# Values, projection and resampling of a second attention in halves, and the next batch's keys through another PSUM bank

## The chip, the cores and the metric

One core of a Trainium2 chip runs the whole program in one launch. The metric is device time in microseconds (us), lower is better. The engines are TensorE (PE in the profile; PEld its weight loads), VectorE (DVE), ScalarE (ACT), GpSimd (POOL) and SyncE (SP, which issues DMAs). Each engine runs its own stream of instructions in order, and the streams are tied together by semaphores.

## What is computed

The reference is a chain of layers over x of shape (4, 256, 256): a conditioned attention, a second attention, a resampling along the channels, a sparsified feed-forward, a GRU over time, a third attention and a routed feed-forward. The change touches the second attention and the resampling behind it:

```python
def _L0_attn_ref(x, W_qkv, W_out, b_out):
    B, S, H = x.shape
    ...
    q8, q_scale = act_quant(q)
    k8, k_scale = act_quant(k)
    scores = jnp.einsum('bhqd,bhkd->bhqk', q8.astype(jnp.float32), k8.astype(jnp.float32))
    scores = scores * (q_scale * k_scale) / jnp.sqrt(jnp.float32(hd))
    attn = jax.nn.softmax(scores, axis=-1)
    v8, v_scale = act_quant(v)
    out = jnp.einsum('bhqk,bhkd->bhqd', attn, v8.astype(jnp.float32))
    out = out * v_scale
    out = out.transpose(0, 2, 1, 3).reshape(B, S, H)
    return jnp.einsum('bsh,ho->bso', out, W_out) + b_out
...
x = x + _L0_attn_ref(_L0_cond_ref(...), L0_attn_W_qkv, L0_attn_W_out, L0_attn_b_out)
x = x + _L0_ffn_ref(_L0_cond2_ref(x, cond_2048, 1, 1), ...)
```

act_quant rounds to an 8-bit float with one scale for the whole tensor. There are 4 batches of 256 tokens and 16 heads of size 16. `_L0_cond2_ref` interpolates linearly between two channels, at places that the condition gives; the kernel does it as a product with a 256x256 matrix for each batch.

## The kernel before

Every engine has one function for the second attention (`phase2_pe`, `phase2_act`, `phase2_pool`, `phase2_dve`), and the order of each stream is written out by hand: a loop over H, the head counted over all batches (0 to 63), with conditions on h = H % 16, the head in its batch b. Some lines ahead of H run 8 heads early (LEAD = 8).

On TensorE, one step H issues, in this order:

- `scores(H + 8)`: two 16-bit products (L938, 32 rows of the array) into one of three banks. VectorE's `top` takes their maxima (L1204, into nraw).
- `by_key(H)`: the same scores with the keys on the partitions (L962), into one of two banks. ScalarE takes the exponential (L1098) into one of eight buffers, work or probs_b. A bank is free again when its exponential is done, so `by_key(H)` waits for the exponential of H-2.
- `rows_again` at H % 4 = 2: two transposes (L948) into bank pY, which bring the queries of the next four heads (a group) back with their maxima beside them. It waits for GpSimd's `split` of that group's maxima (L1156 to L1159). VectorE copies the result out (`rows_out`, L1210), and the group's `by_key` waits for that.
- `values` at H % 4 = 1: probabilities times values of the group before, 8 products of 32-bit numbers (L975) into pR.
- `heads_in(b + 1, side)` at h = 0 (queries) and 2 (keys): 8 transposes each (L924) into pX, copied out by ScalarE's `heads_out` (L1062).
- the chain of the batch before: `out_rows` at h = 3 and 5 (transposes, L990), `out_cols` at h = 7 (L997), `projected` at h = 9 (8 passes of 32-bit product, L1013) and `resample` at h = 12 (L1005). All go through pX. Between them VectorE normalises (L1215, L1218), ScalarE copies (L1077) and VectorE adds the projection to xT (L1224); ScalarE's `regather` copies the resampling out (L1072).

After the loop the last batch's values, output chain and resampling follow, and then the next stage (L1325), which needs all four batches. `keep_warm(n, bank)` issues n products of zeros (L307).

GpSimd's stream in a batch is `split` of the four groups, with the rounding of the next batch's queries, keys and values between them (`pushed`, `rounded_v`, `rounded_qk`); VectorE makes the bit masks for it (`exponents`, L1196 and L1197).

## Time and profile before

| | us |
|---|---|
| median of 3 timed runs | 1082.24 (1080.93 to 1088.04) |
| profiled execution, its own time | 1084.97 |
| its span | 1083.2 |
| TensorE busy in the span | 855.8 (79%) |
| VectorE, ScalarE, GpSimd busy | 674.9, 494.8, 391.7 |
| second attention, from the first by-key product to the next stage | 213.18 to 314.96 |

The times are of whole executions; the span is the part that the profile covers. The second attention is about a tenth of it. The other stages are the same in both kernels.

### The profile page before, as it was taken

Reading aid. Unit: us, or ns where it says so; the run is one execution under the profiler, and the core shown is the slowest. Engines: PE = TensorE matmul, PEld = TensorE weight load, DVE = VectorE, ACT = ScalarE, POOL = GpSimd, SP = SyncE. Lnnn points to the kernel's source line nnn. Section 1 sums busy time; section 2 is a strip of 40 time slices with the busy share of each in tenths; the row PEclk is TensorE's granted clock in tenths of the full one; section 3 lists DMA queues with packets and bytes.
Section 4 is the critical chain, followed back from the end, with each engine's and each line's share of the span. In section 5 each row is a group of like instructions: output and inputs, shape, how many; then the busy total and the mean of one; then the engine's idle time right before and its main releaser. Section 6 shows DMA issues by size and latency. Waiting matters only on the chain.

```text
span 1083.2 us, 39645 instructions
## 1 busy us (share of the span) xinstructions
PE 855.8 (79%) x16359; PEld 544.3 (50%) x16359; DVE 674.9 (62%) x2314; ACT 494.8 (46%) x1987; POOL 391.7 (36%) x473
## 2 busy tenths in 40 slices
PE   3778777788989786969688796967766899999717
PEld 3444443344545464546455464645444567667506
DVE  5644544756434576676667676666766567667573
ACT  2423333456531465656565465655555435435201
POOL 0476550454316294674829285670020000000000
PEclk9999999959899898999999899999999899999768
DMA  8000000400000000000000000000200000000101
GB/s 258 6 1 1 2 1 1 145 2 2 1 20 8 6 6 11 4 14 4 14 4 13 4 4 13 5 14 4 51 34 4 2 1 0 0 0 0 40 0 39
DMA packets 32519, 20.00 MB, mean 18 GB/s; under 512 B 23136, under 2 KB 29280, under 8 KB 32352
## 3 DMA queue, kind: packets, MB, share of 16 engines
q1 hardware_dynamic: 27168, 17.04, 5.6%
q8 instruction: 123, 2.02, 0.8%
q10 hardware_dynamic: 5184, 0.59, 0.4%
q14 instruction: 44, 0.36, 0.1%
HBM read 14.47 MB, written 1.05 MB: 14 GB/s over the span
## 4 chain that ended last, share of the span: by engine, by line
PE 59%; DVE 23%; ACT 7%; issue 6%; POOL 0%; DMA 0%; ACTq 0%; DVEq 0%; POOLq 0%
PE banks L1378 15%; PE banks L1325 5%; PE banks L322 4%; DVE work L1661 4%; DVE gate_r L1657 4%; DVE h_ring L1675 3%; PE banks L1348 3%; ACT nzh L1507 3%; DVE pre_n L1666 3%; PE banks L1690 3%; PE banks L307 3%; PE banks L336 2%; PE banks L551 2%; PE banks L523 2%; PE banks L975 2%
## 5 line engine op out<-in xcount | busy, mean ns | idle before, releaser
L1378 PE MATMUL banks<-w_qkv,h_ring 128*4 128x64 f32 x12288 | 228.1, 223 | 111.0 <-DVE h_ring L1675 98.2
L1378 PEld LDWEIGHTS banks<-w_qkv,h_ring 128*4 128x4 f32 x12288 | 178.5, 89 | 214.4 <-DVE h_ring L1675 197.2
L1498 ACT ACTIVATE banks<-gate_r 128x8 f32<-128x8 f32 x256 | 46.2, 180 | 182.0 <-DVE gate_r L1657 182.0
L307 PE MATMUL banks<-zero 128*128 128x512 bf16 x360 | 113.0, 395 | 2.0 <-PE banks L461 2.0
L1657 DVE STREAM_TRANSPOSE gate_r<-banks 128x64 f32<-128x64 f32 x256 | 64.0, 250 | 79.3 <-PE banks L1378 75.5
L1661 DVE STREAM_TRANSPOSE work<-banks 128x64 f32<-128x64 f32 x256 | 76.6, 299 | 2.9 <-PE banks L1378 2.6
L1675 DVE TENSOR_TENSOR_SCAN h_ring<-banks,nzh 128x24 f32<-128x24 f32 x256 | 52.9, 207 | 32.4 <-ACT nzh L1507 0.8
L1666 DVE TENSOR_TENSOR_SCAN pre_n<-banks,work 128x16 f32<-128x16 f32 x256 | 48.7, 190 | 26.9 <-DVE work L1661 0.9
L1668 DVE STREAM_TRANSPOSE banks<-gate_z 128x64 f32<-128x64 f32 x256 | 60.4, 236 | 6.0 <-ACT gate_z L1503 4.8
L1532 POOL TENSOR_TENSOR work<-work 128x512 f32<-128x512 f32 x14 | 17.8, 1271 | 125.1 <-ACT work L1435 125.1
L1503 ACT ACTIVATE gate_z<-banks 128x64 f32<-128x64 f32 x256 | 57.1, 223 | 11.0 <-PE banks L1378 10.6
L1507 ACT ACTIVATE nzh<-pre_n 128x8 f32<-128x8 f32 x256 | 54.5, 213 | 15.7 <-DVE pre_n L1666 1.0
L375 ACT ACTIVATE probs_b<-banks,nraw 128x128 f32<-128x128 f32 (+1 forms) x128 | 46.8, 417 | 32.5 <-DVE nraw L386 31.5
L1204 DVE TENSOR_REDUCE nraw<-banks 128x2 f32<-128x512 f32 x64 | 42.6, 687 | 29.1 <-PE banks L938 29.1
L322 PE MATMUL banks<-shared,qT 128*128 128x128 f32 (+1 forms) x256 | 59.1, 343 | 0.0
L1458 ACT COPY banks<-big 128x64 f32<-128x64 f32 x256 | 54.1, 211 | 9.3 <-DMA big<-big 9.3
L307 PEld LDWEIGHTS banks<-zero 128*128 128x128 bf16 x360 | 34.1, 98 | 42.4 <-issue 10.5
L1458 ACT COPY banks<-grids 128x64 f32<-128x64 f32 x256 | 54.0, 211 | 0.0
L1458 ACT COPY banks<-bhn 128x64 f32<-128x64 f32 x256 | 54.0, 211 | 0.0
L1625 DVE TENSOR_TENSOR nzh<-h_ring,banks 128x16 f32<-128x16 f32 x256 | 43.9, 171 | 12.2 <-ACTq L1494 3.0
L1603 POOL COPY xnT<-h_ring 128x128 f32<-128x128 f32 x16 | 7.2, 482 | 122.0 <-DVE h_ring L1675 122.0
L1726 POOL COPY aT<-xnT 128x256 f32 (+1 forms) x10 | 3.7, 400 | 117.7 <-PE banks L1690 117.4
(394 smaller groups left out, 1820.2 us busy)
## 6 DMA issues: line engine op xcount, KB each, us to landing
big<-in_x SPq DMA_DIRECT2D x1, 1024.0 KB, 5.8
w_gate<-in_L_ffn_w_gate SPq DMA_DIRECT2D x1, 1024.0 KB, 5.0
shared<-in_L_ffn_w_down SPq DMA_DIRECT2D x1, 1024.0 KB, 7.6
w_gate<-in_L_ffn_W SPq DMA_DIRECT2D x1, 1024.0 KB, 7.0
shared<-in_L_ffn_W SPq DMA_DIRECT2D x1, 1024.0 KB, 6.6
out_x<-big SPq DMA_DIRECT2D x4, 256.0 KB, 2.2
w_qkv<-in_L_cond_W_qkv SPq DMA_DIRECT2D x1, 768.0 KB, 7.0
w_qkv<-in_L_attn_W_qkv SPq DMA_DIRECT2D x1, 768.0 KB, 8.7
```

Of the source, the lines that this page charges most:

```text
L307: nc.tensor.matmul(bank[:, :], zero16[:, 0:P], zero16[:, :], start=True, stop=True, skip_group_check=True)
L322: nc.tensor.matmul(pSQ[h % 3][:, o:o + n], qT[:, c, tile], k[:, c, 0:n], start=True, stop=False, skip_group_check=True)
L1325: mm = nc.tensor.matmul(bank[:, :], xg[:, tile, k, :], w_gate[:, k, n * 512:(n + 1) * 512] if not up else w_up[2 * k + n], start=(k == 0), ...
L1378: mm = nc.tensor.matmul(bank[32 * j:32 * j + B, 0:64], h_col(t, c), w_hh[:, c, g, :].rearrange("p (m n) -> p m n", m=KC)[:, :, 32 * j:32 * ...
L1458: return nc.scalar.copy(bank[:, 0:64], rows).then_inc(done, 1)
L1503: nc.scalar.activation(gate_z[:, :], bank_z[:, 0:64], ACT.Sigmoid, scale=-1.0).then_inc(g_sz, 1)
L1507: nc.scalar.activation(every(nzh[:, :], 0, 3), every(pre_n[:, :], 1), ACT.Tanh, scale=-1.0).then_inc(g_th, 1)
L1657: nc.vector.transpose(gate_r[:, :], bank_r[:, 0:64]).then_inc(g_tr, 1)
L1661: nc.vector.transpose(blocks(npair[:, 16 * (t % RING):16 * (t % RING) + 128], 0), bank_n[:, 0:64].rearrange("p (m n) -> p m n", m=KC)).the ...
L1666: nc.vector.tensor_tensor_scan(pre_n[:, :], zr[:, :], npair[:, 16 * (t % RING):16 * (t % RING) + 16], 0.0, ALU.mult, ALU.add).then_inc(g_p ...
L1668: nc.vector.transpose(blocks(zz[:, :], 2, 3), gate_z[:, :].rearrange("p (m n) -> p m n", m=KC)).then_inc(g_tz, 1)
L1675: nc.vector.tensor_tensor_scan(h_ring[:, h_at(t + 1):h_at(t + 1) + 24], zz[:, 0:24], nzh[:, :], 0.0, ALU.mult, ALU.subtract).then_inc(g_h, 1)
```

## The change

In the second attention:

- `values`, `projected` and `resample` are issued in two halves, under two neighbouring heads: values at H % 4 = 1 and 2, projection at h = 11 and 12, resampling at h = 7 and 8.
- The keys of the next batch come in at h = 3 in place of 2, and through pY (the bank of the rows), after VectorE's copy of the group's rows. `rows_again` of the third group waits for ScalarE's copy of the keys.
- The output chain of the batch before begins two heads later: out_rows at h = 5 and 7, out_cols at h = 9.
- Resampling is done for the batch two before, from batch 2 on, into pY. So the resamplings of batches 2 and 3 both stand after the loop, the first of them in place of three warm-up products. `rows_again` of the fourth group waits for its copy.
- The lead-in has one warm-up product in place of two under heads 4 to 7.
- In batch 0 GpSimd takes `split` of the second group ahead of the rounding of values; VectorE's masks move from h = 2 to 1 and from 8 to 11.

The diff, without most of its unchanged lines:

```diff
@@ -912,12 +912,13 @@
 
...
             def heads_in(b, side):
-                pe.wait_ge(p_qk, b + 1)
-                if side and b:
-                    pe.wait_ge(p_tc, 2 * b + 1)
-                elif b >= 3:
-                    pe.wait_ge(e_xgc, b - 2)
-                out = pR if side and b == 0 else pX
+                out = (pR if b == 0 else pY) if side else pX
+                if side == 0:
+                    pe.wait_ge(p_qk, b + 1)
+                    if b >= 3:
+                        pe.wait_ge(p_x, b - 2)
+                elif b:
+                    pe.wait_ge(a_re, Q + 4 * b - 2)
                 for g in range(4):
...
                         h0 = side * NH + 4 * g
@@ -933,7 +934,8 @@
                     pe.wait_ge(a_max, Q + H - 2)
...
                     pe.wait_ge(p_tc, 2 * b + 2)
-                keep_warm(2 if H < LEAD else 0, bank[H % 3])
+                if H < LEAD:
+                    keep_warm(2 if H < 4 else 1, bank[H % 3])
                 for t in range(ST):
...
                                           start=True, stop=True, skip_group_check=True)
@@ -944,6 +946,10 @@
                 pe.wait_ge(p_split, G + 1)
...
                     pe.wait_ge(a_re, Q + G)
+                if g == 2 and b + 1 < B:
+                    pe.wait_ge(p_tc, 2 * b + 4)
+                if g == 3 and b >= 2:
+                    pe.wait_ge(e_xgc, b - 1)
                 for t in range(ST):
...
                                              ident16[:, :])
@@ -963,26 +969,27 @@
                                           start=True, stop=True, skip_group_check=True)
...
 
-            def values(G):
+            def values(G, t):
                 b, g = divmod(G, 4)
-                pe.wait_ge(a_exp, Q + 4 * G + 4)
-                if g == 0:
-                    pe.wait_ge(p_v8, b + 1)
-                if g % 2 == 0 and G:
-                    pe.wait_ge(a_oqc, 2 * B + G // 2)
-                for t in range(ST):
-                    for j in range(4):
-                        mm = nc.tensor.matmul(pR[32 * j:32 * j + 32, (g % 2) * S:(g % 2 + 1) * S], vs[b % 2][:, t, 4 * g + j, :],
-                                              prob[(4 * G + j) % 8][:, t * S:(t + 1) * S], start=(t == 0), stop=(t == ST - 1), skip_group_check=True)
-                mm.then_inc(a_v, 1)
+                if t == 0:
+                    pe.wait_ge(a_exp, Q + 4 * G + 4)
+                    if g == 0:
+                        pe.wait_ge(p_v8, b + 1)
+                    if g % 2 == 0 and G:
+                        pe.wait_ge(a_oqc, 2 * B + G // 2)
+                for j in range(4):
+                    mm = nc.tensor.matmul(pR[32 * j:32 * j + 32, (g % 2) * S:(g % 2 + 1) * S], vs[b % 2][:, t, 4 * g + j, :],
+                                          prob[(4 * G + j) % 8][:, t * S:(t + 1) * S], start=(t == 0), stop=(t == ST - 1), skip_group_check=True)
+                if t == ST - 1:
+                    mm.then_inc(a_v, 1)
 
...
                     if b + 2 < B:
-                        pe.wait_ge(p_tc, 2 * b + 6)
+                        pe.wait_ge(p_tc, 2 * b + 5)
                     else:
-                        pe.wait_ge(e_xgc, b)
+                        pe.wait_ge(p_x, b)
                 elif b + 1 < B:
...
                 out = bank[0] if t and b == B - 1 else pX
@@ -997,22 +1004,26 @@
                         mm = nc.tensor.transpose(pX[:, c * S + t * P:c * S + (t + 1) * P], o_sb[:, t, c * P:(c + 1) * P], ident)
...
 
-            def resample(b, out):
-                pe.wait_ge(e_gm, b + 1)
-                pe.wait_ge(p_x, b + 1)
-                for m in range(KC):
-                    for k in range(KC):
-                        mm = nc.tensor.matmul(out[:, m * S:(m + 1) * S], gmats[b][:, k, m * P:(m + 1) * P], xT[:, k, b * S:(b + 1) * S],
-                                              start=(k == 0), stop=(k == KC - 1), skip_group_check=True)
-                mm.then_inc(e_xg, 1)
-
-            def projected(b):
-                pe.wait_ge(a_otc, B + b + 1)
-                for m in range(KC):
-                    for k in range(KC):
-                        mm = nc.tensor.matmul(pX[:, m * S:(m + 1) * S], w_out2[:, k, m * P:(m + 1) * P], oT[:, k, :],
-                                              start=(k == 0), stop=(k == KC - 1), skip_group_check=True)
-                mm.then_inc(p_proj, 1)
+            def resample(b, out, m):
+                if m == 0:
+                    pe.wait_ge(e_gm, b + 1)
+                    pe.wait_ge(p_x, b + 1)
+                    if b + 2 < B:
+                        pe.wait_ge(a_re, Q + 4 * b + 11)
+                for k in range(KC):
+                    mm = nc.tensor.matmul(out[:, m * S:(m + 1) * S], gmats[b][:, k, m * P:(m + 1) * P], xT[:, k, b * S:(b + 1) * S],
+                                          start=(k == 0), stop=(k == KC - 1), skip_group_check=True)
+                if m == KC - 1:
+                    mm.then_inc(e_xg, 1)
+
+            def projected(b, m):
+                if m == 0:
+                    pe.wait_ge(a_otc, B + b + 1)
+                for k in range(KC):
+                    mm = nc.tensor.matmul(pX[:, m * S:(m + 1) * S], w_out2[:, k, m * P:(m + 1) * P], oT[:, k, :],
+                                          start=(k == 0), stop=(k == KC - 1), skip_group_check=True)
+                if m == KC - 1:
+                    mm.then_inc(p_proj, 1)
 
...
             nc.tensor.transpose(pX[0:3, 0:P], amax3[:, :], ident).then_inc(s_gmax, 1)
@@ -1031,27 +1042,32 @@
                     by_key(H)
...
                     rows_again((H + 2) // 4)
-                if H % 4 == 1 and H > 4:
-                    values(H // 4 - 1)
-                if b >= 0 and b + 1 < B and h in (0, 2):
-                    heads_in(b + 1, h // 2)
-                if b >= 1 and h in (3, 5):
-                    out_rows(b - 1, (h - 3) // 2)
-                if b >= 1 and h == 7:
+                if H % 4 in (1, 2) and H > 4:
+                    values(H // 4 - 1, H % 4 - 1)
+                if b >= 0 and b + 1 < B and h in (0, 3):
+                    heads_in(b + 1, h // 3)
+                if b >= 1 and h in (5, 7):
+                    out_rows(b - 1, (h - 5) // 2)
+                if b >= 2 and h in (7, 8):
+                    resample(b - 2, pY, h - 7)
+                if b >= 1 and h == 9:
                     out_cols(b - 1)
-                if b >= 1 and h == 9:
-                    projected(b - 1)
-                if b >= 1 and h == 12:
-                    resample(b - 1, pX)
-            values(4 * B - 1)
-            keep_warm(3, bank[1])
+                if b >= 1 and h in (11, 12):
+                    projected(b - 1, h - 11)
+            for t in range(ST):
+                values(4 * B - 1, t)
+            for m in range(KC):
+                resample(B - 2, bank[3], m)
             for t in range(ST):
...
             out_cols(B - 1)
-            projected(B - 1)
+            keep_warm(3, bank[1])
+            for m in range(KC):
+                projected(B - 1, m)
             keep_warm(6, bank[1])
-            resample(B - 1, pY)
+            for m in range(KC):
+                resample(B - 1, pY, m)
             pe.wait_ge(e_xg, B)
...
             phase3_pe(pe)
@@ -1059,7 +1075,7 @@
         def phase2_act(act):
...
                 act.wait_ge(p_t, 2 * b + side + 1)
-                nc.scalar.copy((qT16s, kT16s)[side][b % 2].rearrange("p g s -> p (g s)"), pX.bitcast(BF16)).then_inc(p_tc, 1)
+                nc.scalar.copy((qT16s, kT16s)[side][b % 2].rearrange("p g s -> p (g s)"), (pX, pY)[side].bitcast(BF16)).then_inc(p_tc, 1)
 
...
                 act.wait_ge(a_v, Q + 4 * b + 2 * n + 2)
@@ -1096,17 +1112,18 @@
                 if H >= 8:
...
                 nc.scalar.activation(prob[H % 8], bank[3 + H % 2], ACT.Exp, scale=sscale[:, 0:1]).then_inc(a_exp, 1)
-                if b + 1 < B and h in (0, 2):
-                    heads_out(b + 1, h // 2)
-                if b >= 1 and h == 1:
+                if b + 1 < B and h in (0, 3):
+                    heads_out(b + 1, h // 3)
+                if b >= 1 and h == 2:
                     out_of_groups(b - 1, 1)
-                if h == 9:
+                if b >= 2 and h == 8:
+                    regather(b - 2, pY)
+                if b >= 1 and h == 9:
+                    out_cols_out(b - 1)
+                if h == 10:
                     out_of_groups(b, 0)
-                if b >= 1 and h == 7:
-                    out_cols_out(b - 1)
-                if b >= 1 and h == 12:
-                    regather(b - 1, pX)
             out_of_groups(B - 1, 1)
+            regather(B - 2, bank[3])
             out_cols_out(B - 1)
...
             regather(B - 1, pY)
@@ -1164,16 +1181,20 @@
                 split(4 * b)
...
                     pushed(0, 2, 3)
-                    rounded_v(0)
-                if b + 1 < B:
+                elif b + 1 < B:
                     pushed(b + 1, 2, 3)
                 split(4 * b + 1)
-                if b + 1 < B:
+                if b == 0:
+                    rounded_v(0)
+                    pushed(1, 2, 3)
+                elif b + 1 < B:
                     rounded_v(b + 1)
...
                 split(4 * b + 3)
+                if b == 0:
+                    rounded_v(1)
                 if b + 2 < B:
...
             pool.wait_ge(p_v8, B)
@@ -1258,15 +1279,15 @@
                 if H in (-6, -3):
...
                     exponents((H + 6) // 3, 2, 3, p_ev)
-                if b >= 0 and b + 2 < B and h == 2:
+                if b >= 0 and b + 2 < B and h == 1:
                     v.wait_ge(p_y, b + 2)
                     exponents(b + 2, 0, 2, p_e)
-                if b >= 0 and b + 2 < B and h == 8:
+                if b >= 0 and b + 2 < B and h == 11:
                     v.wait_ge(p_yv, b + 3)
                     exponents(b + 2, 2, 3, p_ev)
-                if b >= 1 and h in (4, 6):
-                    out_normalised(b - 1, (h - 4) // 2)
-                if b >= 1 and h == 10:
+                if b >= 1 and h in (6, 8):
+                    out_normalised(b - 1, (h - 6) // 2)
+                if b >= 1 and h == 13:
                     projected_out(b - 1)
...
```

TensorE's stream in batch 1, before, from the second `out_rows` to the values under head 9 (L938 scores, L962 by key, L948 rows, L990 and L997 transposes of the output, L975 values):

```order
199 L990 MATMUL banks<-cst,work 128x128 x4
200 L938 MATMUL banks<-shared,qT 128x256 x2
201 L962 MATMUL banks<-shared 128x256 x2
202 L948 MATMUL banks<-ident,qkp 128x128 x2
203 L938 MATMUL banks<-shared,qT 128x256 x2
204 L962 MATMUL banks<-shared 128x256 x2
205 L997 MATMUL banks<-cst,o_sb 128x128 x4
206 L938 MATMUL banks<-shared,qT 128x256 x2
207 L962 MATMUL banks<-shared 128x256 x2
208 L938 MATMUL banks<-shared,qT 128x256 x2
209 L962 MATMUL banks<-shared 128x256 x2
210 L975 MATMUL banks<-probs_b,work 32x256 x8
```

The changed kernel, same batch, from the rows under head 6 to out_cols (L940 scores, L968 by key, L954 rows, L997 and L1004 transposes, L981 values):

```order
205 L954 MATMUL banks<-ident,qkp 128x128 x2
206 L981 MATMUL banks<-work 32x256 x4
207 L940 MATMUL banks<-shared,qT 128x256 x2
208 L968 MATMUL banks<-shared 128x256 x2
209 L997 MATMUL banks<-cst,work 128x128 x4
210 L940 MATMUL banks<-shared,qT 128x256 x2
211 L968 MATMUL banks<-shared 128x256 x2
212 L940 MATMUL banks<-shared,qT 128x256 x2
213 L968 MATMUL banks<-shared 128x256 x2
214 L981 MATMUL banks<-probs_b,work 32x256 x4
215 L1004 MATMUL banks<-cst,o_sb 128x128 x4
```

The values stood whole under heads 5 and 9, with both transposes between; now a half stands under head 6 too, and out_cols follows the half under head 9.

TensorE's stream after the last head, before (L1325 is the next stage):

```order
308 L975 MATMUL banks<-probs_b,work 32x256 x8
309 L307 MATMUL banks<-zero 128x512 x3
310 L990 MATMUL banks<-cst,work 128x128 x8
311 L307 MATMUL banks<-zero 128x512 x3
312 L997 MATMUL banks<-cst,o_sb 128x128 x4
313 L1013 MATMUL banks<-oT,w_out 128x256 x4
314 L307 MATMUL banks<-zero 128x512 x6
315 L1005 MATMUL banks<-xT,h_ring 128x256 x4
316 L1325 MATMUL banks<-w_gate,xnT 128x512 x2
```

The changed kernel there (L1014 resampling, L1023 projection, L1346 the next stage):

```order
330 L981 MATMUL banks<-probs_b,work 32x256 x8
331 L1014 MATMUL banks<-xT,h_ring 128x256 x4
332 L997 MATMUL banks<-cst,work 128x128 x8
333 L307 MATMUL banks<-zero 128x512 x3
334 L1004 MATMUL banks<-cst,o_sb 128x128 x4
335 L307 MATMUL banks<-zero 128x512 x3
336 L1023 MATMUL banks<-oT,w_out 128x256 x4
337 L307 MATMUL banks<-zero 128x512 x6
338 L1014 MATMUL banks<-xT,h_ring 128x256 x4
339 L1346 MATMUL banks<-w_gate,xnT 128x512 x2
```

The resampling of batch 2 took the place of the first three warm-up products, and three more stand ahead of the projection.

GpSimd's stream in batch 0, before, from the first group's split on (L1156 to L1159 split, L1131 and L1147 values):

```order
53 L1159 TENSOR_TENSOR qkp<-nraw,qkp 128x2x4
54 L1131 TENSOR_TENSOR big<-big,grids 128x256 x2
55 L1147 TENSOR_TENSOR v_sb<-big,grids 128x16x16 x2
56 L1131 TENSOR_TENSOR big<-big,grids 128x256 x2
57 L1156 TENSOR_TENSOR qkp<-nraw,zero 128x2x4
```

The changed kernel there (L1173 to L1176 split, L1148 and L1164 values):

```order
53 L1176 TENSOR_TENSOR qkp<-nraw,qkp 128x2x4
54 L1148 TENSOR_TENSOR big<-big,grids 128x256 x2
55 L1173 TENSOR_TENSOR qkp<-nraw,zero 128x2x4
56 L1174 TENSOR_TENSOR nraw<-nraw,qkp 128x2x4
57 L1175 TENSOR_TENSOR qkp<-nraw,zero 128x2x4
58 L1176 TENSOR_TENSOR qkp<-nraw,qkp 128x2x4
59 L1164 TENSOR_TENSOR v_sb<-big,grids 128x16x16 x2
```

The second split moved ahead of two of the three pieces of work on the values.

## Rows read from the trace of the kernel before

**Rows 1.** Stretches: batches 0 to 3 and tail; us, busy (instructions), PEclk

```profile
213.18:235.64 22.46, 18.24 (x139) 7.77 (x139) 14.20 (x25) 12.27 (x19) 14.65 (x29) 0.59 0.01 1
235.64:260.78 25.14, 22.93 (x181) 12.50 (x180) 15.42 (x31) 14.91 (x23) 11.45 (x25) 0.82 0.01 1
260.78:283.40 22.62, 20.41 (x183) 11.91 (x182) 13.14 (x27) 14.12 (x23) 4.99 (x18) 0.92 0.00 1
283.40:303.86 20.46, 17.39 (x145) 9.10 (x141) 8.12 (x18) 12.85 (x21) 9.56 (x14) 0.92 0.01 2
303.86:314.96 11.10, 9.19 (x57) 5.66 (x57) 2.27 (x6) 3.24 (x5) 0.71 (x1) 1.00 0.00 1
```

**Rows 2.** Waits of TensorE in batch 2: total us, times, longest

```profile
PE banks L997 <- DVE o_sb L1218: 0.7, 1, 0.7
PE banks L990 <- ACT shared L1062: 0.7, 1, 0.7
PE banks L1005 <- DVE xT L1224: 0.4, 1, 0.4
PE banks L990 <- DVE o_sb L1218: 0.2, 1, 0.2
```

**Rows 3.** Timeline of TensorE in batch 0: start, us, what, idle before

```profile
217.01 0.28 PE L948 MATMUL banks<-ident,qkp 128*128 128x128 bf16 x2 [2.28 <-POOL qkp L1159]
...
225.34 0.60 PE L962 MATMUL banks<-shared 32*128 32x256 bf16 x2 [0.59 <-ACT probs_b L1098]
```

**Rows 4.** Timeline of TensorE in batches 1 and 2

```profile
243.20 0.40 PE L938 MATMUL banks<-shared,qT 32*128 32x256 bf16 x4
...
243.75 1.07 PE L975 MATMUL banks<-work 128*32 128x256 f32 x16
...
249.53 1.94 PE L975 MATMUL banks<-probs_b,work 128*32 128x256 f32 x16
...
261.87 1.07 PE L975 MATMUL banks<-probs_b,work 128*32 128x256 f32 x16
...
263.53 0.61 PE L924 MATMUL banks<-ident,qkp 128*128 128x128 bf16 x8
...
266.44 1.07 PE L975 MATMUL banks<-work,v_sb 128*32 128x256 f32 x16
...
271.53 1.70 PE L975 MATMUL banks<-probs_b,v_sb 128*32 128x256 f32 x16
273.16 3.00 PE L1013 MATMUL banks<-oT,w_out 128*128 128x256 f32 x8
...
278.34 1.96 PE L1005 MATMUL banks<-xT,w_emb 128*128 128x256 f32 x8 [0.40 <-DVE xT L1224]
```

**Rows 5.** Stretches of half a microsecond in which the clock changes

```profile
217.00:217.50 0.50, 0.49 (x7) 0.49 (x8) 0.17 (x1) 0.00 (x0) 0.50 (x1) 0.72 0.00 0
...
241.00:241.50 0.50, 0.50 (x8) 0.38 (x7) 0.50 (x2) 0.20 (x2) 0.02 (x1) 0.89 0.00 0
...
247.50:248.00 0.50, 0.31 (x3) 0.31 (x4) 0.50 (x2) 0.23 (x1) 0.00 (x0) 0.94 0.00 0
...
271.50:272.00 0.50, 0.50 (x10) 0.31 (x12) 0.50 (x1) 0.50 (x2) 0.34 (x3) 0.83 0.00 0
...
292.00:292.50 0.50, 0.50 (x7) 0.14 (x5) 0.15 (x1) 0.20 (x1) 0.23 (x1) 0.81 0.00 0
```

**Rows 6.** Timeline of TensorE behind the last values

```profile
304.86 0.82 PE L307 MATMUL banks<-zero 128*128 128x512 bf16 x3
```

**Rows 7.** Timeline of GpSimd in batch 0: split of the second group

```profile
215.82 0.23 POOL L1156 TENSOR_TENSOR qkp<-nraw,zero 128x8 bf16<-128x8 f32 x1
```

**Rows 8.** Groups of VectorE, 205 to 315: busy us, mean ns, idle before

```profile
L1204 DVE TENSOR_REDUCE nraw<-banks 128x2 f32<-128x512 f32 x64 | 42.6, 687 | 29.1 <-PE banks L938 29.1
...
L1218 DVE SCALAR_TENSOR_TENSOR o_sb<-banks,scl,rinv 128x256 f32<-128x256 f32 x8 | 3.9, 484 | 0.3
...
L1196 DVE TENSOR_SCALAR grids<-big 128x1024 int32<-128x1024 int32 x2 | 1.4, 682 | 0.0
```

## The prediction

> **What bounds the kernel now.** The change touches only the second attention, so I first cut its stretch of the span into its four batches with the table of stretches [rows 1]. Its columns give each engine's busy time and, as PEclk, the mean share of full clock that TensorE was granted: 1.00 is 2.4 GHz, 0.50 is 1.2 GHz. In every batch TensorE is the busiest engine by far: 22.93 of 25.14 us in batch 1, against 15.42 on VectorE and 14.91 on ScalarE. What isn't busy on TensorE is 4.2, 2.2, 2.2 and 3.1 us in batches 0 to 3. The list of waits splits batch 2's: 0.7 + 0.7 + 0.4 + 0.2 = 2.0 us, all of them on the side chain (rows of the output, columns, projection, resampling), none on the exponentials [rows 2]. So the bound inside the batches is TensorE's own work, plus these waits.
>
> The second thing that the table shows is the clock. It averages 0.59, 0.82, 0.92 and 0.92. A stretch of length T at mean clock c holds T(1-c) of lost time if TensorE is busy throughout: 22.46 x 0.41 = 9.2 us in batch 0, 25.14 x 0.18 = 4.5 in batch 1, 22.62 x 0.08 = 1.8 in batch 2, 20.46 x 0.08 = 1.6 in batch 3. Together 17.1 us, more than all waits. Fine stretches place it [rows 5]: the clock falls near 217, is back near 241, and falls again near 248, 272 and 292.
>
> What did TensorE do before a fall? The timeline says [rows 4]: values (L975, 32-bit, 1.07 us at full clock) start at 243.75 and next at 249.53; between their end and the next start lie 4.7 us of 16-bit products and transposes, and the clock fell in them. Between 267.5 and 271.53 it is 4.0 us: it fell. Between 262.9 and 266.44 it is 3.5 us: it didn't. The fall at 292 lies in the same part of batch 3: between the values of heads 5 and 9, where a batch has its transposes of the output and one of its two longest waits. The fall at 217 follows 2.28 us without any work, in which TensorE waited for GpSimd's split of the second group's maxima [rows 3].
>
> **The change part by part.**
>
> *Values in halves.* The work is the same, in two pieces under neighbouring heads. At full clock two heads' scores and products by key take 0.55 us (243.20 to 243.75, [rows 4]) and one whole values block 1.07. The products by key run at most two heads ahead of the exponentials, so a whole block leaves ScalarE without input, and TensorE then waits for ScalarE: 0.59 us at 225.34 [rows 3], about once in each group of batch 0. The list of waits of batch 2 has no exponential in it, so the halves save no wait there. The cost of a split is the start of one more block: a block lasts 1.07 us where its steady part is 1.00, so 0.07 for each of some seven splits in a batch: +0.5 us. Below zero is excluded there, since no wait is named that it could remove; above, a split also parts two heads that now overlap (two heads 0.55 us, a head alone about 0.54 to 0.55 with its fill), at most 7 x 0.25 = 1.8 us more. I take 0.5, as most heads of a batch already have a block between them.
>
> *Keys through pY, later output chain.* The keys' transposes no longer go through pX, so the first out_rows needn't wait for ScalarE's copy of the keys: -0.7 us in batches 1 and 2 [rows 2]. out_cols now stands behind half a values block (0.53 us) and, in batches 2 and 3, behind half a resampling: its 0.7 us wait goes in those and falls to about 0.2 in batch 1. Resampling no longer follows the projection that it had to see through VectorE: -0.4. out_rows of the second tile keeps its wait; VectorE's chain from the scores of head 14 (maximum 0.69, product 0.48 [rows 8], and two short operations between them, some 1.8 us in all) against TensorE's 1.45 in between (0.55 for head 15, 0.55 for what is left of head 14, 0.3 of rows and 0.5 of values, less the overlap) gives about 0.35 in place of 0.2. New waits: the keys' transposes at head 3 wait for VectorE's copy of the group's rows, and the bit masks of batches 2 and 3 (two passes of 0.68 us [rows 8]) now stand ahead of that copy in batches 0 and 1: some 0.5 us in batch 1 at full clock. ScalarE waits for the second half of resampling before it goes on to the exponential of head 9; ScalarE has 8 us of slack in a batch (14.1 of 22.6 busy [rows 1]), so I cost that at nothing; without that cover it is 0.35 us in each of two batches. Sum of waits: batch 1 -1.0, batch 2 -1.6, batch 3 -1.2 (it has no heads to bring in; 0.7 of out_cols and 0.2 of the resampling go, and part of the 1.3 us for the last exponentials).
>
> *Resampling two batches late.* One block of 1.96 us [rows 4] leaves batch 1 and lands in the tail: batches 2 and 3 still carry one each. Batch 1: -2.0. In the tail it takes the place of three warm-up products (0.82 us, [rows 6]) between the last values and out_rows, which could start no earlier since they waited for ScalarE's copy of the last groups: 1.96 - 0.82 = +1.15, and +0.1 for the warm-up products now ahead of the projection: +1.25. The end of this stage, 314.96 [rows 1], is what the next stage waits for, so all of it counts.
>
> *Clock in the batches.* In batch 1 the changed stream has between the second values half (head 6) and the next half (head 9): three heads at 0.55, one block of transposes (0.6, as the keys' at 263.53) and its wait of 0.35, that is 2.6 us. Between heads 2 and 5 it is three heads and the keys' transposes (0.6), 2.3 us. In batches 2 and 3 two halves of resampling fill heads 7 and 8. No stretch without 32-bit products is as long as any after which the clock fell, or as the 3.5 us after which it didn't, so I expect the falls of batches 1 to 3 to go: -1.7, -1.7 and -1.6. The long one of batch 0 follows the 2.28 us without work. GpSimd now does split(1) ahead of the values' rounding; it started at 215.82 [rows 7] and could start at about 213.8, when VectorE has its maximum. But VectorE's masks, moved up to head 1, take 1.4 us [rows 8] before the copy of the rows, so the keys' transposes and by-key products of the second group come at about 217.4 as before, and TensorE is idle for some 2 us there all the same; and four heads of the lead-in lose half of their warm-up products. So that fall stays. In half-clock stretches TensorE gained only where full-array 32-bit work and transposes stood close, as at 241; with two heads_in blocks and two halves within heads 0 to 3 of batch 1, this can come earlier. Batch 1 now has 5.4 us at half clock at its start (235.64 to 241), 2.7 us of them lost: the term lies between 0 and -2.7, I take -0.9, nearer to no change, as batch 0's values alone never brought it back.
>
> *Batch 0.* The 0.59 us waits for the exponentials go in part, and the 2.28 us wait is partly replaced: between 0 and -2.5, I take -0.6, the size of one such wait.
>
> **The sum.** Batch 0 -0.6. Batch 1: -1.0 -2.0 -1.7 -0.9 +0.5 = -5.1. Batch 2: -1.6 -1.7 +0.5 = -2.8. Batch 3: -1.2 -1.6 +0.5 = -2.3. Tail +1.25. Total -9.5 us. On the profiled execution's own 1084.97 us that is 1075.5. This execution lies 2.7 above the median of the three timed ones, 1082.24; from the median it is 1072.7. I predict 1073.
>
> **The rivals.**
>
> *The falls stay* (chance 0.22). The stretch before a fall may be counted otherwise than by its 32-bit products: the values at 261.87 and 266.44 lay in a stretch as thin as the one that fell. Then the terms -1.7, -1.7, -1.6 and -0.9 go, and 3.6 us are left: 1078.6. For it: ahead of the falls at 248 and 272 TensorE did stand still for 0.7 us [rows 2]. Against it: the spacing of the three falls. The Trainium skill ("TensorE: Matmul & The Clock Gate", section on why this matters for your kernels) ties a lower clock to long idle gaps between bursts of products; by that rule no fall here is explained, since the clock falls after idle of 0.7 us at most in batches 1 and 2, and rearranging busy work would give this rival's 1078.6.
>
> *The clock does better* (0.18). If TensorE, getting its rows for the second group some 2 us earlier, doesn't fall at 217, or is back in the middle of batch 0, half of that batch's 9.2 us is saved: 1073 - 4.6 = 1068. Against: the idle time ahead of 217.4 as worked out.
>
> *New waits eat the old* (0.12). pY now serves rows, keys and resampling; each change of hands crosses VectorE or ScalarE. With the 1.8 us of parted heads in place of 0.5 in one or two batches and 0.35 to 0.5 us per hand-over, 4 us are lost: 1077.
>
> *Slower* (0.08). The halves thin out TensorE's stream, so the clock, once down in batch 0, isn't granted again at 241. Batch 1's work is 25.14 - 2.2 (waits) - 4.5 (clock) - 2.0 (resampling) = 16.4 us at full clock; done at half clock it costs 16.4 more, where the forecast has 1.8 and the waits of 1.2 vanish: +13.4, 1086. It decides against the change from about 11 us of work at half clock, which is about head 10 of batch 1. If batch 2's 18.6 us run so too, it is 1103. Against: the projection, now in halves at heads 11 and 12, is as dense as at 273, where the clock came back.
>
> **How the numbers follow.** The forecast has 0.40. Its own spread, from the bounds above, is about 1068 to 1079. A measurement of this kernel can't tell changes of less than about 1%, 10.8 us: below 1071.4 is faster, above 1093 slower. Faster: all but a little of the better clock (0.16) and 0.18 of the forecast's 0.40, 0.34. Slower: 0.05, the part of the slower case that runs on into batch 2, and a little of the new waits. The rest, 0.61, is within 1%. For 8 in 10 the range runs from the better clock with a margin, 1064, to short of the slower case, 1083.
>
> **What the changed profile would show.** Mean clock of batches 1 to 3 above 0.95 and no fall between heads 5 and 9 (clock term right); idle time of TensorE near 1.2, 0.4 and 1.9 us (waits right); the stage's last resampling some 12.4 us behind the last exponential's end in place of 11.2 (tail right). A clock still at half at head 8 of batch 1, or idle time ahead of the keys' transposes, would make the prediction wrong.

## The result, and the profile after

The changed kernel took 1112.94 us (median of 4, 1111.88 to 1116.07), the kernel before beside it 1085.14. The ratio is 1.0257, 95% interval [1.0197, 1.0316]: 28 us slower, where 9 us less were forecast. Ratios here and below leave out executions more than 1.5% above the fastest of the same kernel; medians and ranges keep them. The profiled execution took 1111.88, its span is 1110.1.

The same table of stretches as [rows 1], cut at the same places of the program (batches 0 to 3, then past the stage's end at 340.09):

```profile
213.00:235.62 22.62, 19.58 (x138) 7.34 (x138) 14.58 (x25) 12.38 (x18) 15.38 (x29) 0.51 0.01 2
235.62:266.73 31.11, 31.09 (x174) 13.73 (x173) 16.60 (x31) 14.19 (x21) 11.72 (x25) 0.50 0.00 1
266.73:298.12 31.39, 31.39 (x152) 15.06 (x150) 11.66 (x22) 13.51 (x20) 4.93 (x18) 0.50 0.00 1
298.12:327.99 29.87, 27.56 (x174) 11.66 (x173) 11.14 (x23) 14.85 (x23) 9.55 (x14) 0.65 0.00 1
327.99:340.00 12.01, 10.79 (x63) 7.19 (x64) 2.27 (x6) 3.83 (x6) 0.61 (x1) 1.00 0.00 1
```

The clock is 0.50 in batches 1 and 2 and 0.65 in batch 3, where it was 0.82, 0.92 and 0.92. Batch 0 is as long as before. TensorE is busy for all of the 31.39 us of batch 2: no wait is left in the list, only slow work (the ends of products are modelled in the profile, so busy doesn't mean at its peak). The list of waits of TensorE for 213 to 328:

```profile
PE banks L968 <- ACT work L1114: 1.5, 2, 0.8
PE banks L968 <- ACT probs_b L1114: 1.5, 2, 0.8
PE banks L925 <- DVE shared L1231: 1.5, 1, 1.5
PE banks L968 <- DVE shared L1231: 1.1, 1, 1.1
PE banks L981 <- ACT probs_b L1114: 0.8, 1, 0.8
```

None of the waits of [rows 2] is there; the 1.5 us wait for VectorE ahead of the keys' transposes in batch 0 is the one that the prediction feared. Half-microsecond stretches give the fall and the return, as in [rows 5]:

```profile
213.00:213.50 0.50, 0.50 (x6) 0.29 (x7) 0.50 (x2) 0.07 (x1) 0.00 (x0) 0.99 0.00 0
213.50:214.00 0.50, 0.50 (x8) 0.47 (x5) 0.50 (x2) 0.50 (x1) 0.23 (x2) 0.50 0.00 0
...
319.00:319.50 0.50, 0.50 (x3) 0.32 (x1) 0.00 (x0) 0.00 (x0) 0.50 (x1) 0.70 0.00 0
319.50:320.00 0.50, 0.50 (x4) 0.11 (x2) 0.00 (x0) 0.19 (x1) 0.50 (x2) 1.00 0.00 0
```

So the clock was at 1.2 GHz from 213.5 to 319, 106 us, against some 34 before (217 to 241, and three falls). The timeline of TensorE in batch 2 shows the densest work that didn't bring it back (L1014 resampling behind transposes, L1023 projection), and in batch 3 what it had just done when it came back (L1014 again):

```profile
280.19 1.11 PE L997 MATMUL banks<-cst,work 128*128 128x128 f32 x4
281.10 1.91 PE L1014 MATMUL banks<-xT,w_emb 128*128 128x256 f32 x4
...
283.90 2.08 PE L1014 MATMUL banks<-xT,w_emb 128*128 128x256 f32 x4
...
292.19 2.08 PE L1023 MATMUL banks<-oT,w_out 128*128 128x256 f32 x4
294.20 0.60 PE L940 MATMUL banks<-shared,qT 32*128 32x256 bf16 x2
294.60 0.63 PE L968 MATMUL banks<-shared 32*128 32x256 bf16 x2
295.15 2.08 PE L1023 MATMUL banks<-oT,w_out 128*128 128x256 f32 x4
...
314.75 1.11 PE L997 MATMUL banks<-cst,work 128*128 128x128 f32 x4
315.66 1.91 PE L1014 MATMUL banks<-xT,w_emb 128*128 128x256 f32 x4
317.50 0.60 PE L968 MATMUL banks<-shared 32*128 32x256 bf16 x2
318.04 1.74 PE L1014 MATMUL banks<-xT,w_emb 128*128 128x256 f32 x4
```

The same transposes and halves of the resampling stood in batch 2 without a return and in batch 3 ahead of one. So what TensorE had just done doesn't settle by itself when the clock comes back.

The stage ends at 340.09 in place of 314.96, 25.1 us later. The rest of the program is 770.0 us long, 768.2 before.

### The profile page after: what moved, and what is told of

Its sections match the earlier page's. It is cut to its first block, busy times and chain, and to the rows that moved or that the text cites. A ratio compares the mean times of both kernels' runs of the same rounds, so it can differ in the third digit from the quotient of the medians.

```text
span 1110.1 us, 39535 instructions
## 1 busy us (share of the span) xinstructions
PE 855.6 (77%) x16255; PEld 550.9 (50%) x16355; DVE 678.0 (61%) x2314; ACT 496.3 (45%) x1987; POOL 392.3 (35%) x473
## 4 chain that ended last, share of the span: by engine, by line
PE 60%; DVE 20%; ACT 6%; issue 5%; SPq 2%; DMA 2%; ACTq 0%; DVEq 0%; POOL 0%; POOLq 0%
PE banks L1399 13%; PE banks L1346 5%; PE banks L322 4%; DVE work L1682 3%; PE banks L1369 3%; DVE h_ring L1696 3%; DVE gate_r L1678 3%; PE banks L981 3%; ACT nzh L1528 3%; PE banks L1711 3%; PE banks L307 3%; DVE pre_n L1687 2%; SPq L1326 2%; PE banks L336 2%; PE banks L940 2%
## 5 line engine op out<-in xcount | busy, mean ns | idle before, releaser
L307 PE MATMUL banks<-zero 128*128 128x512 bf16 x256 | 74.8, 392 | 3.9 <-PE banks L461 2.6
```

The costliest lines, as they stand in the source:

```text
L307: nc.tensor.matmul(bank[:, :], zero16[:, 0:P], zero16[:, :], start=True, stop=True, skip_group_check=True)
```

## The experiments

Each line of measurement gives the median, the ratio to the kernel before on the same chip with its interval, and from the profiled execution where the clock changed and where the stage ended (first product of the next stage). The profile shows one execution only; for the others there is the mean clock of the whole program.

### Which half does it

The changed kernel with whole values:

```diff
-                if H % 4 in (1, 2) and H > 4:
-                    values(H // 4 - 1, H % 4 - 1)
+                if H % 4 == 1 and H > 4:
+                    for t in range(ST):
+                        values(H // 4 - 1, t)
```

> The changed kernel, but the values of a group are issued whole again under H % 4 = 1 (projection and resampling stay in halves). Theory A: it is the values' halves that keep the clock down, since 1.87 us of 32-bit products in a row at half clock, next to the transposes of the keys or queries, were what stood ahead of the clock's return at 241 in the kernel before. Then the clock is back in batch 1, near 241, the mean clock of batch 1 is 0.75 or more, and the time is 1075 to 1090. Theory B: it is the projection and the resampling, taken apart or taken out of batch 1; then this kernel stays at half clock to batch 3, 1108 to 1118. Theory C: the clock stays down because the lead-in has fewer warm-up products and the fall comes earlier; then this one too stays near 1112.

Measured 1083.72 us, 0.9983 [0.9926, 1.0040]; fall at 213, return at 247, a second fall from 284.5 to 288, stage end 312.99. Theory A's return came; theory C fell, since the first fall was as early and the lead-in the same.

The changed kernel with whole projection and resampling:

```diff
-                if b >= 2 and h in (7, 8):
-                    resample(b - 2, pY, h - 7)
+                if b >= 2 and h == 7:
+                    for m in range(KC):
+                        resample(b - 2, pY, m)
...
-                if b >= 1 and h in (11, 12):
-                    projected(b - 1, h - 11)
+                if b >= 1 and h == 11:
+                    for m in range(KC):
+                        projected(b - 1, m)
```

> The changed kernel, but the projection is issued whole under head 11 and the resampling whole under head 7 (values stay in halves). Theory A (values' halves alone): no return before the projection of batch 1; if the whole projection (4 us at half clock) brings it back, near 262, the time is 1090 to 1100, and if not 1112. Theory B (projection and resampling in halves): the clock is back at the projection of batch 1, 1085 to 1098. Theory C (lead-in): 1112.

Measured 1086.31 us, 0.9974 [0.9934, 1.0014]; return at 261.5, a second fall at 288.5 with the clock back only at 298.5, stage end 318.51 (this profiled execution was the longest of the eight, 1094.84). So neither kind of halves keeps the clock down by itself: with blocks of either kind whole it came back. The mean clocks of all executions say the same: 0.934 to 0.948 with whole values, 0.927 to 0.945 with whole projection and resampling, against 0.904 to 0.915 in the changed kernel.

The kernel before with halved values (ScalarE's copies of them come one head later, which isn't shown here):

```diff
-                if H % 4 == 1 and H > 4:
-                    values(H // 4 - 1)
+                if H % 4 in (1, 2) and H > 4:
+                    values(H // 4 - 1, H % 4 - 1)
```

> The kernel before, with the values alone in halves under H % 4 = 1 and 2 (and ScalarE's copies of them one head later). Theory A: the clock doesn't return at 241; the whole projection of batch 1 may bring it back some 15 us later. Half clock for 15 us more costs about 7 us: 1088 to 1097, or 1110 if it stays down. Theory B and theory C: as before, the clock returns at 241 and the time is 1080 to 1088.

Measured 1098.69 us (2 runs), 1.0128 [0.9893, 1.0362], which settles no difference in time; in the profile the return moved from 241 to 262.5, just behind the whole projection of batch 1 (3.78 us from 257.94), the clock fell twice more (276 to 286.5 and 296.5 to 310), and the stage ended at 329.20. The late return alone proves little: further down, a kernel with whole values has its first return at 260. What the three returns had behind them, in the timelines of whole values (first), whole projection (second) and the kernel before with halved values (third):

```profile
243.71 1.93 PE L981 MATMUL banks<-work 128*32 128x256 f32 x16
245.57 1.12 PE L997 MATMUL banks<-cst,work 128*128 128x128 f32 x4
```

```profile
256.55 3.78 PE L1023 MATMUL banks<-oT,w_out 128*128 128x256 f32 x8
```

```profile
257.94 3.78 PE L1014 MATMUL banks<-oT,w_out 128*128 128x256 f32 x8
```

The reader is to compare them with the projection above: the same products, 2.08 us twice with 1.0 us of 16-bit products on 32 rows between, gave no return.

### Is the clock the whole loss

12 more warm-up products in the changed kernel, in batch 0:

```diff
+                if H == 12:
+                    keep_warm(12, bank[H % 3])
```

> The changed kernel with 12 more warm-up products in a row ahead of the scores of head 12, some 5 us at half clock in batch 0. If the clock is the whole loss: it comes back near 223, the schedule of the change then runs at full clock, and the time is 1065 to 1078, under the kernel before. If thin work also makes it fall again (the halves are too thin to hold it), the mean clock of batches 1 to 3 stays under 0.8 and the time is 1090 or more.

Measured 1115.15 us (2 runs), 1.0280 [1.0108, 1.0451]. The clock did come back, at 224, and held with halves for 10 us; then TensorE waited 1.51 us for GpSimd's split of batch 1's first group, the clock fell at 234 and came back at 319.5; the stage ended at 341.06:

```profile
224.50:234.00 9.50, 7.26 (x88) 2.88 (x84) 7.98 (x13) 7.42 (x12) 5.52 (x11) 1.00 0.01 2
234.00:234.50 0.50, 0.00 (x0) 0.00 (x0) 0.50 (x2) 0.03 (x1) 0.36 (x2) 0.87 0.00 0
234.50:319.50 85.00, 83.14 (x448) 36.80 (x448) 39.83 (x74) 35.62 (x53) 22.58 (x59) 0.50 0.00 1
```

The same burst at the start of batch 1:

```diff
+                if H == 24:
+                    keep_warm(12, bank[H % 3])
```

> The changed kernel, all halves kept, with 12 more warm-up products in a row at the start of batch 1 (ahead of the scores of head 24), some 5 us at half clock. The burst in batch 0 brought the clock back at 224, but it fell again at 234, where TensorE waited 1.5 us for GpSimd, and the halves then didn't bring it back. Theory (halves can't win the clock back, but can hold it): here it is back near 241 and stays to the end of the stage, mean clock of batches 2 and 3 over 0.95; the time is 1076 to 1086. Rival (halves can't hold it either): another fall in batch 1 or 2 without a wait of 1 us ahead of it, and 1100 or more.

Measured 1085.73 us, 0.9953 [0.9912, 0.9994]; return at 240.5, no fall for the rest of the stage, end 311.79, though the burst itself took 5.0 us:

```profile
240.50:241.00 0.50, 0.50 (x3) 0.00 (x0) 0.00 (x0) 0.00 (x0) 0.00 (x0) 0.83 0.00 0
241.00:311.79 70.79, 66.02 (x563) 35.46 (x563) 40.05 (x79) 44.66 (x69) 26.10 (x54) 1.00 0.00 1
```

One burst of zeros takes back all 28 us. With the clock up, the same halves kept it for 70 us; with the clock down, they went 85 us (burst in batch 0) and 106 us (no burst) without it. That they can never win it back isn't shown: both returns near 319 came in halves.

The same with 8 products in place of 12 (`keep_warm(8, bank[H % 3])`):

> The changed kernel with a burst of 8 warm-up products at the start of batch 1 in place of 12. If the return needs only some 3 us of full-array products together with the transposes behind them: as with 12, 1.5 us less, 1078 to 1086. If 8 are too few: no return before batch 3, 1110 to 1116.

Measured 1085.58 us, 0.9948 [0.9909, 0.9987]; return at 239, end 310.17. Three of its ten executions were more than 1.5% above the fastest: 1099.76 and 1101.33 us at mean clocks of 0.933 and 0.922, and 1119.43 us at 0.905, like the changed kernel. In that one 8 products seem not to have been enough; it has no profile.

### What the order is worth without the halves

The changed kernel with values, projection and resampling all whole (both diffs above):

> The changed kernel's order and banks, but values, projection and resampling all whole (heads H % 4 = 1, 11 and 7). Theory (the halves are the whole loss, the rest of the change is worth a little): 1078 to 1088, the clock back at 241 to 247, the stage's end within 3 us of the run with the values whole alone. Rival (the new order itself costs): 1092 or more with the same clock as the kernel before.

Measured 1084.39 us (3 runs), 0.9938 [0.9863, 1.0014]; return at 247, one fall from 261 to 267.5, end 312.11. The new order without the halves shows no cost.

Whole up to head 31, halves behind it:

```diff
+                if H < 2 * NH:
+                    for t in range(ST):
+                        if H % 4 == 1 and H > 4:
+                            values(H // 4 - 1, t)
+                elif H % 4 in (1, 2):
+                    values(H // 4 - 1, H % 4 - 1)
...
-                if b >= 1 and h in (11, 12):
+                if b == 1 and h == 11:
+                    for m in range(KC):
+                        projected(b - 1, m)
+                elif b >= 2 and h in (11, 12):
```

> The changed kernel with the values whole up to head 31 and the projection whole in batch 1, in halves afterwards. Theory (halves are harmful only while the clock is down): the clock is back at 241 to 247 as with whole values, holds, and the time is 1076 to 1084. Rival (halves make the clock fall again and then keep it down): mean clock of batch 2 or 3 under 0.8, 1090 or more.

Measured 1087.07 us, 0.9959 [0.9913, 1.0005]; return at 248, a fall at 261, a return at 275, then no fall, end 316.45. The fall came less than 1 us behind the start of the first half (260.43), at the place where the kernel with everything whole fell too. Neither branch came out as put. Ahead of the return at 275 stood only halves and transposes (at half clock 1.11 us of transposes from 271.40 and 1.91 us of resampling from 272.30), so in this profile work in halves did win the clock back, 14 us after the fall.

### Waits and thin work

The kernel before with four warm-up products under head 7 of batches 1 to 3:

```diff
-                keep_warm(2 if H < LEAD else 0, bank[H % 3])
+                keep_warm(2 if H < LEAD else 4 if H >= NH and h == 15 else 0, bank[H % 3])
```

> The kernel before with four more warm-up products under head 7 of batches 1 to 3, ahead of the transposes that wait 0.7 us for VectorE. Theory (each fall near 248, 272 and 292 follows thin work between heads 5 and 9, and costs some 1.6 us): the falls go, each burst costs 0.2 to 0.9 us, so 1080 to 1084 and mean clock of batches 2 and 3 over 0.97. Rival (the falls follow the place of the batch in time, not the work): they stay, and the time is 1086 to 1090.

Measured 1090.12 us, 0.9972 [0.9925, 1.0019]: no difference. In the profile the first return came late, at 260, but behind it no fall followed to the stage's end at 318.82. Up to 249.5 this kernel issues the same work as the kernel before, with all its whole values blocks, yet its clock did not come back at 241. Lines of its timeline:

```profile
245.44 1.94 PE L975 MATMUL banks<-work 128*32 128x256 f32 x16
247.31 1.12 PE L990 MATMUL banks<-cst,work 128*128 128x128 f32 x4
...
249.50 1.91 PE L307 MATMUL banks<-zero 128*128 128x512 bf16 x4
...
256.19 3.78 PE L1013 MATMUL banks<-oT,w_out 128*128 128x256 f32 x8
```

The first two are what the return with whole values had behind it (243.71 and 245.57 there), and here none came. So a whole values block makes a return likelier at best; it doesn't assure one.

The kernel before with its waits filled, 4 products ahead of the scores of head 8, 9 under head 2, 4 under head 7:

```diff
-                keep_warm(2 if H < LEAD else 0, bank[H % 3])
+                keep_warm(2 if H < LEAD else 4 if H == LEAD or H >= NH and h == 15 else 0, bank[H % 3])
...
+                if H == 2:
+                    keep_warm(9, pR)
```

> The kernel before with warm-up products in its waits: 4 ahead of the scores of head 8, 9 under head 2 ahead of the rows that waited 2.3 us for GpSimd, 4 under head 7 of batches 1 to 3. Theory: the fall at 217 goes as well, 1076 to 1084, some 3 to 5 us above the changed kernel that is held in the same way, for the waits that the change removes. Rival (the fall at 217 comes all the same): 1085 to 1091.

Measured 1090.62 us, 0.9995 [0.9956, 1.0034]: no difference. The profile (the longest of its ten executions, 1098.84) shows no fall at 217, but one at 227.5 and 24 us at half clock; the stage ended at 311.97.

The changed kernel with the waits of batch 0 filled:

```diff
+                if H == 8:
+                    keep_warm(5, bank[H % 3])
...
+                if H == 14:
+                    keep_warm(7, pX)
...
+                if H == 3:
+                    keep_warm(7, pR)
```

> The changed kernel with warm-up products in the three waits of batch 0: 5 ahead of the scores of head 8, 7 under head 3 ahead of the transposes that wait 1.5 us for VectorE, 7 under head 14 ahead of the rows that waited 1.5 us for GpSimd where the clock was up. Theory (the halves hold a clock that isn't let down, and the falls follow waits and thin work): no fall at 213 nor at 234, mean clock of the second attention over 0.9, the stage's end near 307 in place of 314.96, 1074 to 1082. Rival (batch 0 is too thin even so): it falls somewhere in batch 0 and isn't back before batch 3, 1105 to 1118.

Measured 1077.00 us, 0.9884 [0.9818, 0.9950], the lowest median of the study. One line for the whole stage (205 to its end at 301.06): the clock never fell.

```profile
205.00:301.00 96.00, 88.24 (x748) 43.97 (x746) 62.21 (x116) 58.14 (x91) 48.12 (x96) 1.00 0.03 10
```

The same with everything whole:

> The kernel that holds the clock from the start (warm-up products in the waits of batch 0), but with values, projection and resampling whole. If the clock holds here too, the difference to it is what the halves themselves are worth at full clock: a whole block of values keeps ScalarE waiting some 0.15 us longer in a group, a split costs 0.07; so the stage's end lies within 1.5 us of 301.1, and the time is 1074 to 1082. If the halves are what holds the clock between heads 5 and 9, it falls once or twice in batches 1 to 3, and the time is 1079 to 1088.

Measured 1082.95 us (12 runs), 0.9929 [0.9887, 0.9972]; end 306.32. One of the twelve took 2033.48 us at a mean clock of 1.000; nothing on record explains it. The warm-up products carried it to 241; then the clock fell, and again at 279, each time just behind the start of the values block that ends a stretch of thinner work (240.97 and 278.06). The first of them:

```profile
236.19 1.07 PE L983 MATMUL banks<-work 128*32 128x256 f32 x16
...
239.83 0.66 PE L999 MATMUL banks<-cst,work 128*128 128x128 f32 x4 [0.69 <-DVE o_sb L1248]
...
240.97 1.69 PE L983 MATMUL banks<-probs_b,work 128*32 128x256 f32 x16
```

With halves in the same place (the timeline of the kernel above) the same work is spread, and nothing fell in that one profile:

```profile
235.81 0.64 PE L983 MATMUL banks<-work 128*32 128x256 f32 x8
...
237.72 0.64 PE L983 MATMUL banks<-work 128*32 128x256 f32 x8
...
240.15 0.64 PE L983 MATMUL banks<-probs_b,work 128*32 128x256 f32 x8
```

In time the two held kernels aren't told apart: their intervals overlap, and so do their executions (1072.19 to 1082.27 in halves, 1070.29 to 1089.43 whole, the one above aside). What the halves themselves are worth at full clock is open.

## Why the prediction was wrong

**What bounds the kernel** was read rightly: TensorE's work and its clock. Batch 0's term (-0.6) came to +0.2 (22.46 to 22.62), and its long fall stayed, 3.5 us earlier (213.5 for 217).

**The step that failed** is the clock at the start of batch 1, "between 0 and -2.7, I take -0.9". It took for granted that the return at 241 would come at all and asked only whether it came sooner. In [rows 4] the values block at half clock is 1.94 us in a row. The change cuts it into two of 1.08, and cuts the projection, the next block that could do it, into two of 2.08. With both cut, the clock stayed down for 106 us; with either one whole it came back (247, 261.5), and with 12 zero products in a row as well (240.5). That the return at 241 was not safe even without the change is shown by the kernel before with warm-up products under head 7, where it came at 260. This was the rival "slower", with its mechanism right, its price right in kind (1086 for batch 1 alone, 1103 with batch 2; it went on into batch 3, 1113) and its chance of 0.08 far too low. What was held against it, that the projection in halves "is as dense as at 273", is refuted by 292.19 to 297.16.

**The forecast's other clock terms** (-1.7, -1.7, -1.6, the falls in batches 1 to 3 go) came true where everything was in halves and the clock had been brought back or held: no fall behind the two bursts in batch 1, nor in the kernel held from the start. The burst in batch 0 held the clock only up to a wait of 1.51 us. They didn't where only the values were in halves: the clock fell at 288.5 with whole projection and resampling, and at 276 and 296.5 in the kernel before. With everything whole in the last kernel two falls came. The picture of the longest stretch without 32-bit products is only a part: the fall at 279 had 2.7 us between blocks, less than the 3.5 that did no harm in [rows 4].

**The terms of work and waits** can be checked where the clock was up. In the kernel held from the start, the first values half under head 1 starts at 231.89, 250.73 and 271.03 in batches 1 to 3 and the last block at 288.95, 12.1 us ahead of the stage's end. In the kernel before these are 237.56, 261.87, 284.23, 303.86 and 11.1. So batch 1 went from 24.3 to 18.8 (forecast -5.1, measured -5.5), batch 2 from 22.4 to 20.3 (-2.8, -2.1), batch 3 from 19.6 to 17.9 (-2.3, -1.7), and the tail rose by 1.0 (forecast 1.25).

The waits were forecast well. TensorE's idle time in these three stretches is 2.2, 2.5 and 2.8 us before and 1.1, 0.8 and 1.7 in the held kernel, so -1.1, -1.7 and -1.1 against -1.0, -1.6 and -1.2. The time at half clock before, halved, is an estimate of the clock's part: 3.5, 1.7 and 1.7 us. With these and the 2.0 us of resampling taken out, what is left, for splitting the blocks above all, is an estimate of about +1.1, +1.3 and +1.1, where the forecast has +0.5 in each batch. That term was too small. The prediction read 0.07 for a split. At full clock a whole values block starts at 231.77 in the last kernel and the next work 1.00 later; in the held kernel the work behind each half starts 0.57 later (231.89 and 232.46), so a split costs 0.14. The projection goes from 1.93 (268.35 to 270.28) to twice 1.06 (243.91 to 244.97), +0.19. And two heads parted cost 0.54 twice in place of 0.55 together, so 0.5 for each pair, where the bound took 0.25.

**Busy and still slow.** TensorE was busy for 31.39 of 31.39 us at half clock, and 83 of 85 in the run with the early burst. The Trainium skill ("TensorE: Matmul & The Clock Gate", section on why this matters for your kernels) advises to keep TensorE busy without gaps for the fast clock. The trace doesn't agree for this kind of work: busy with products on 32 rows and short 32-bit blocks, it stayed at 1.2 GHz. The rival that the prediction set beside this page of the Trainium skill, that the falls stay and nothing else changes (1078.6), was wrong too.

**What stays open.** How much of which work the clock wants isn't settled; the runs only order cases, and one and the same work stood with a return and without. What lets it fall isn't either. Each fall behind batch 0 that was looked at (248, 272 and 292 in the kernel before, 284.5, 288.5, 276, 296.5, 261, 241 and 279 in the others) came during a wait of 0.6 to 0.9 us on TensorE or up to 2.2 us behind one, so short waits are as good a candidate as thin work; but waits of 0.67 and 0.77 us in the held kernel (ahead of 270.71 and 274.31) brought no fall. No run parts the two.

The kernel held from the start ends the stage 13.9 us earlier in its profile than the kernel before, but its span is only 6.8 shorter: the rest of the program took 775.3 us in place of 768.2. Other falls there are not the whole of it. Added up over stretches of 4 us, the time lost to half clock in the rest is 37.4 us before and 40.9 in the held kernel, 3.5 more; and in the kernel with 12 products in batch 1 it is 37.6, 0.2 more than before, while its rest took 774.1.

## What to carry to other kernels

Before work on TensorE is split and spread, look for where the profile's granted clock rises and what stood right before. A change that breaks up all such blocks can leave most of a stage at 1.2 GHz while TensorE hardly waits. Don't rely on one return in one profile: the same work had it at 241 once and not before 260 another time. Here a dense burst behind the fall, or warm-up products in the waits in which the clock would fall, made up for it. What a split costs is read from start to start of the blocks and their neighbours, not from the block's length alone. When a rival turns on a state of the chip, price how long the state can last, not only one step of it.

## What the runs showed of the hardware that I had not expected

- The clock stayed at 1.2 GHz for 106 us. In 83.4 us of them (235.6 to 319) TensorE was busy for 81.9. The mean clock of all four executions of the changed kernel, 0.904 to 0.915, says that none was much better.
- 12 warm-up products of zeros, 5.2 and 5.0 us long, mostly at half clock, had it back by their end in both profiles (224 and 240.5).
- From batch 1 on, the changed kernel's halves ran for 83 us at half clock without getting the fast one back, and behind the burst for 71 us at the fast one without losing it: the same stream, at either level.
- Executions of one and the same kernel before went from 1082.06 us at a mean clock of 0.946 to 1100.01 at 0.930 on one chip. Span times what is missing from full clock gives an estimate of 58 and 77 us lost, as far apart as the two times: the clock differs from one execution to the next, and that can be most of the noise here.
